# Recommendation tower on one core: two features of 26 go from gathers to lookups, and the gathers are released in another place

## The reference

```python
e = jnp.stack([tbl_0[ids[:, 0]], ..., tbl_25[ids[:, 25]]], axis=1)        # (2048, 26, 128)
combined = jnp.concatenate([dense[:, None, :], e], axis=1)                 # (2048, 27, 128)
interactions = jnp.einsum('bfd,bgd->bfg', combined, combined)
z = jnp.concatenate([dense, interactions[:, _IU0, _IU1]], axis=1)
h = jnp.concatenate([z, dense], axis=1)
h = jnp.maximum(h @ W_top1 + b_top1, 0.0)      # (607, 512)
h = jnp.maximum(h @ W_top2 + b_top2, 0.0)      # (512, 256)
y = h @ W_top3                                 # (256, 1)
```

## Time and profile before

| | |
|---|---|
| median of three timed runs | 380.81 us |
| span of the profiled execution | 496.1 us |
| its own time beside the span | not given with this profile |
| TensorE busy | 376.0 us, 3360 matmuls |
| weight loads | 301.4 us |
| DVE busy | 244.4 us |
| ACT busy | 195.0 us |
| GpSimd busy | 254.8 us, 256 of its 266 instructions gathers |
| mean granted TensorE clock | 0.904 of 2.4 GHz |
| moved by DMA | 58.44 MB, 118 GB/s on average |

### The profile page before, as it was taken

The page is one execution under the profiler, slowest core; times in us unless marked ns, Lnnn a source line. Parts: engine busy times, 40 slices in busy tenths (PEclk is TensorE's granted clock), DMA queues, the critical chain, the costliest instruction groups (busy, mean ns, idle before and its releaser), DMA issues.

```text
span 496.1 us, 8109 instructions
## 1 busy us (share of the span) xinstructions
PE 376.0 (76%) x3360; PEld 301.4 (61%) x3360; DVE 244.4 (49%) x174; ACT 195.0 (39%) x261; POOL 254.8 (51%) x266
## 2 busy tenths in 40 slices
PE   1951777858586665978798796969788696879997
PEld 1630656647474554767586666867676455666787
DVE  4740789674919370765725750956566101112133
ACT  3810986414242521525252532434354334344400
POOL 6774540655737363646666554747466564730000
PEclk9985799989989796989998898989899898789899
DMA  8841763259915153456714533536232621123330
GB/s 210 218 134 41 218 187 85 70 156 275 227 29 161 45 155 103 109 150 153 183 46 128 160 87 104 143 93 193 74 89 63 168 73 27 49 63 100 69 71 5
DMA packets 38479, 58.44 MB, mean 118 GB/s; under 512 B 21665, under 2 KB 22561, under 8 KB 38444
## 3 DMA queue, kind: packets, MB, share of 16 engines
q1 hardware_dynamic: 29304, 40.74, 30.3%
q0 software_dynamic: 8192, 16.79, 13.5%
q10 hardware_dynamic: 948, 0.41, 0.4%
HBM read 47.68 MB, written 10.23 MB: 117 GB/s over the span
## 4 chain that ended last, share of the span: by engine, by line
PE 58%; issue 16%; DVE 11%; another core or an unknown queue 8%; SPq 3%; DMA 2%; ACT 2%; DVEq 0%; ACTq 0%
PE look_bank L727 25%; PE short_bank L821 15%; DVE one_hot L1031 8%; PE out_bank L757 6%; PE out_bank L771 4%; PE short_bank L806 4%; PE out_bank L766 3%; SPq L632 2%; DVE all_combined L1044 1%; DVE low_table L1019 1%; DMA spread_ids<-in_ids_by_feature 1%; PE out_bank L783 1%; SPq L621 1%; DMA last_scratch<-all_dots 1%
## 5 line engine op out<-in xcount | busy, mean ns | idle before, releaser
L682 POOL DMA_INDIRECT rows<-in_tbl,all_ids x256 | 253.9, 992 | 191.9 <-PE short_bank L821 81.9
L1031 DVE TENSOR_TENSOR one_hot<-spread_ids,row_bank 128x2048 fp32r<-128x2048 int32 (+3 forms) x80 | 170.7, 2175 | 27.1 <-PE look_bank L727 10.7
L727 PE MATMUL look_bank<-one_hot,high_table 125*128 125x512 f32 x328 | 140.8, 429 | 20.0 <-issue 16.1
L727 PE MATMUL look_bank<-one_hot,low_table 125*128 125x512 f32 x328 | 132.4, 404 | 0.6 <-issue 0.6
L821 PE MATMUL short_bank<-all_combined 128*59 128x54 f32 x2048 | 88.1, 247 | 53.2 <-issue 51.5
L821 PEld LDWEIGHTS short_bank<-all_combined 128*59 128x59 f32 x2048 | 79.7, 162 | 66.7 <-issue 66.5
L1044 DVE COPY all_combined<-short_bank 128x512 f32<-128x512 f32 x32 | 21.8, 691 | 156.2 <-PE short_bank L806 122.3
L727 PEld LDWEIGHTS look_bank<-one_hot,high_table 125*128 125x128 f32 x328 | 64.5, 197 | 40.5 <-issue 23.6
L727 PEld LDWEIGHTS look_bank<-one_hot,low_table 125*128 125x128 f32 x328 | 64.6, 197 | 16.9 <-issue 4.1
L925 ACT COPY all_dots<-short_bank 128x432 f32<-128x432 f32 x64 | 33.1, 518 | 97.1 <-remote 53.7
L878 ACT COPY looked_up<-look_bank 128x512 f32<-128x512 f32 x40 | 23.4, 586 | 120.8 <-remote 45.3
(11 more groups left out here) (42 smaller groups left out, 183.5 us busy)
## 6 DMA issues: line engine op xcount, KB each, us to landing
whole_table<-in_tbl SPq DMA_DIRECT2D x26, 448.0 KB
spread_ids<-in_ids_by_feature SPq DMA_DIRECT2D x40, 256.0 KB
block_scratch<-all_dots SPq DMA_DIRECT2D x24, 208.0 KB
rows<-in_tbl,all_ids POOLq DMA_INDIRECT x256
block_scratch<-all_dots SPq DMA_DIRECT2D x24, 104.0 KB
pairs<-block_scratch SPq DMA_DIRECT2D x72, 29.2 KB
whole_table<-in_tbl SPq DMA_DIRECT2D x26, 52.0 KB
whole_table<-in_tbl SPq DMA_DIRECT2D x2, 560.0 KB
```

What stands on the lines that cost most here:

```text
L682: nc.gpsimd.indirect_dma_start(rows[:, t % ROW_TILES, slot, :], None, tables[SLOT_FEATURES[slot]][:, :], bass.IndirectOffsetOnAxis(ap=all_ ...
L727: last = nc.tensor.matmul(look_bank[s % LOOK_BANKS][:], table_parts[part][TABLE_PLACE[s]][0:ROWS_K, c, :], one_hot[0:ROWS_K, (chunks_befor ...
L1031: last = nc.vector.tensor_tensor(one_hot[:, place:place + n, :], spread_ids[:, s % ID_PLACES:s % ID_PLACES + 1, :].to_broadcast([P, n, COLS]),
```

## The change

Two more features of every block are looked up: 14 gathered, 12 looked up. The order of slots changes so that three tables of 1250 rows are among the twelve. Places shrink to 18 for one-hots and 5 for ids, and grow to 20 for looked-up results. Each tile's stage gets six halves of lookups. The transposes of tile 0 stand behind eight lookups, not four. The groups of slots are 4, 4, 4 and 2. The gathers of tile 2 are released by the transposes of tile 0; behind these a table, `GATHERS_BESIDE`, says how many gathers of the tiles 3 to 15, in order, follow the transposes of tile 1, of tile 2, and so on. No gather waits for dots or for halves of lookups.

```diff
-SLOT_FEATURES = [6, 3, 10, 23, 2, 4, 8, 11, 12, 13, 14, 15, 16, 18, 19, 21, 1, 5, 7, 9, 17, 20, 0, 22, 24, 25]
+SLOT_FEATURES = [6, 3, 10, 23, 2, 4, 8, 11, 12, 13, 14, 15, 16, 18, 1, 5, 7, 19, 9, 17, 20, 21, 22, 24, 25, 0]
-GATHERED = [16, 16, 16, 16]
+GATHERED = [14, 14, 14, 14]
-HOT_PLACES = 20
-ID_PLACES = 7
-LOOK_PLACES = 15
+HOT_PLACES = 18
+ID_PLACES = 5
+LOOK_PLACES = 20
-GROUPS = [[4, 4, 4, 4] for _ in range(BLOCKS)]
+GROUPS = [[4] * (n // 4) + [n % 4] * (n % 4 > 0) for n in GATHERED]
-HALVES_AFTER = [[6, 5, 5, 4] for _ in range(LAST)]
+HALVES_AFTER = [[6, 6, 6, 6], [6, 6, 6, 6], [6, 6, 6, 6]]
-LOOKS_BEFORE_TURN = 4
+LOOKS_BEFORE_TURN = 8
-HIGH_BEFORE_TURN = 6
-HIGH_PAIR = 6
-def high_after(s):
-    if s == HIGH_BEFORE_TURN - SPLIT_AHEAD or s == HIGH_PAIR + 1:
-        return []
-    return [s + SPLIT_AHEAD, s + SPLIT_AHEAD + 1] if s == HIGH_PAIR else [s + SPLIT_AHEAD]
+GATHERS_BESIDE = [11, 11, 11, 11] + [15] * 8 + [10, 8]
+TILES_AT_START, TILES_BEFORE_DOTS = 2, 3
+def gathers_beside(w):
+    rest = [(t, slot) for t in range(TILES_BEFORE_DOTS, TILES) for slot in range(GATHERED[t // PER_BLOCK])]
+    first = sum(GATHERS_BESIDE[:w])
+    return rest[first:first + GATHERS_BESIDE[w]]
...
 def look_place(s):
-    return BLOCK_OF[s] % 2 * (LOOK_PLACES - IN_BLOCK[0]) + LOOK_SLOT[s]
+    return BLOCK_OF[s] % 2 * (LOOK_PLACES - IN_BLOCK[BLOCK_OF[s]]) + LOOK_SLOT[s]
...
-            for t in range(ROW_TILES):
-                gather(t, range(n_groups(t)))
-            for t in range(TILES - ROW_TILES):
-                pool.wait_ge(turned_done, groups_by(t))
-                gather(t + ROW_TILES, range(1))
-                for g in range(1, n_groups(t + ROW_TILES) - 1):
-                    if 0 < t <= LAST * PER_BLOCK:
-                        pool.wait_ge(half_done, halves_beside(t, g))
-                    gather(t + ROW_TILES, range(g, g + 1))
-                pool.wait_ge(dots_done, (t + 1) * FILLS - 1)
-                gather(t + ROW_TILES, range(n_groups(t + ROW_TILES) - 1, n_groups(t + ROW_TILES)))
+            for t in range(TILES_AT_START):
+                gather_tile(t)
+            pool.wait_ge(turned_done, groups_by(0))
+            for t in range(TILES_AT_START, TILES_BEFORE_DOTS):
+                gather_tile(t)
+            for w in range(len(GATHERS_BESIDE)):
+                pool.wait_ge(turned_done, groups_by(w + 1))
+                for t, slot in gathers_beside(w):
+                    gather(t, slot)
```

More of the change, by code:

```diff
@@ L108 @@
 ACT_HOTS = [1, 2, 4, 5, 7, 8]
-LOOKS_BEFORE_TURN = 4
+LOOKS_BEFORE_TURN = 8
 START_IDS_AHEAD = 5
 DENSE_AFTER = 1
-HIGH_BEFORE_TURN = 6
-HIGH_PAIR = 6
-def high_after(s):
-    if s == HIGH_BEFORE_TURN - SPLIT_AHEAD or s == HIGH_PAIR + 1:
-        return []
-    return [s + SPLIT_AHEAD, s + SPLIT_AHEAD + 1] if s == HIGH_PAIR else [s + SPLIT_AHEAD]
+GATHERS_BESIDE = [11, 11, 11, 11] + [15] * 8 + [10, 8]
+TILES_AT_START, TILES_BEFORE_DOTS = 2, 3
+assert sum(GATHERS_BESIDE) == sum(GATHERED[t // PER_BLOCK] for t in range(TILES_BEFORE_DOTS, TILES))
+def gathers_beside(w):
+    rest = [(t, slot) for t in range(TILES_BEFORE_DOTS, TILES) for slot in range(GATHERED[t // PER_BLOCK])]
+    first = sum(GATHERS_BESIDE[:w])
+    return rest[first:first + GATHERS_BESIDE[w]]
 def group_slots(t, g):
@@ L150, in odds_by, with group_of @@
     return sum(n_groups(i) // 2 for i in range(t + 1))
+def group_of(t, slot):
+    return next(g for g in range(n_groups(t)) if slot in group_slots(t, g))
 def turn_use(t, g):
@@ L184, in look_place, with block_before @@
 def look_place(s):
-    return BLOCK_OF[s] % 2 * (LOOK_PLACES - IN_BLOCK[0]) + LOOK_SLOT[s]
+    return BLOCK_OF[s] % 2 * (LOOK_PLACES - IN_BLOCK[BLOCK_OF[s]]) + LOOK_SLOT[s]
+def block_before(s):
+    earlier = [BLOCK_OF[i] for i in range(s) if look_place(i) == look_place(s)]
+    return earlier[-1] if earlier else None
 def chunks_before(s):
@@ L216, in hots_by_dve @@
     return half + 1 - hots_by_act(half)
-def halves_beside(t, g):
-    before = 2 * IN_BLOCK[0] + sum(HALVES_AFTER[i // PER_BLOCK][i % PER_BLOCK] for i in range(t - 1))
-    return before + 1 + (g - 1) * HALVES_AFTER[(t - 1) // PER_BLOCK][(t - 1) % PER_BLOCK] // 2
 def free_places(half):
@@ L678, in _, with gather, gather_tile @@
         def _(pool):
[L679 to L684, removed]
+            def gather(t, slot):
+                nc.gpsimd.indirect_dma_start(
+                    rows[:, t % ROW_TILES, slot, :], None, tables[SLOT_FEATURES[slot]][:, :],
+                    bass.IndirectOffsetOnAxis(ap=all_ids[:, t, slot:slot + 1], axis=0)).then_inc(
+                        gathered[t % ROW_TILES][group_of(t, slot)], 16)
+            def gather_tile(t):
+                for slot in range(GATHERED[t // PER_BLOCK]):
+                    gather(t, slot)
             nc.gpsimd.memset(ones[:], 1.0).then_inc(ones_ready, 1)
@@ L873, in copy_look @@
             def copy_look(s):
-                if s >= LOOK_PLACES:
-                    act.wait_ge(look_moved, moves_by(BLOCK_OF[s - LOOK_PLACES] * PER_BLOCK + PER_BLOCK - 1))
+                if block_before(s) is not None:
+                    act.wait_ge(look_moved, moves_by(block_before(s) * PER_BLOCK + PER_BLOCK - 1))
                 act.wait_ge(half_done, 2 * (s + 1))
@@ L966, in copy_ends @@
                         m = BLOCK_OF[s]
-                        for ahead in high_after(s):
-                            high_part(ahead)
+                        high_part(s + SPLIT_AHEAD)
                         if s == FIRST_MOVES[0] - 1:
@@ L986, in _ @@
             copy_ends(start[:LOOKS_BEFORE_TURN])
-            high_part(HIGH_BEFORE_TURN)
             copy_dense(0)
```

## The result

The changed kernel takes 418.6 us (median of 5 runs, 417.78 to 422.99) against 380.5 us before (378.82 to 381.22). The ratio is 1.1022, with a 95% interval of 1.0968 to 1.1075: 38 us slower. Forecast were 410 us and a range of 393 to 420.

A forecast was written before the change was run, and what follows sets the result against it. TensorE's work and the start were taken to bound the kernel, GpSimd close behind. Lookups +36.4, transposes -4.1, start +4, gather order -8, DVE +1 summed to +29, so 380.8 became 410 us; range 393 to 420.

The forecast's parts named there:

- The ledger of TensorE's work: Kernel before: TensorE's matmuls and transposes, added up from trace rows at full clock, come to 323 us.
- the 53 us and the 81 us: TensorE, kernel before: 53 us of work taking longer and 81 us of issue idle, which timed runs can't have.
- TensorE's work and the start are thus the bound: Kernel before: 323 us of work plus 52 of the other 57 us named, about 5 us unnamed.
- GpSimd was the bound: Rival, kernel before: gathers bind, all 24 us of the loop's idle would go, 396 us; chance 0.24.
- chain of 371 us: GpSimd, kernel before: gathers from the first dots end at 339 us, 31.5 us follow, 10 us under the median.
- Lookups, +36.4: TensorE's lookups: 80 more chunks, 160 matmuls of 0.2275 us, counting in full, +36.4 us.
- Start, +13.1: Up to first dots: DVE's four new halves and two low parts; 9.1 us matmuls, +4 beyond, bounds 0 and +8.
- the 14 us I took out: Start, kernel before: ACT's standstill of 21.65 us for a lookup's copy; without 14 us, first dots at 70.7 us.
- The order of the gathers, -8: Loop: fewer gathers beside dots end stalls; the timed run gets back between 0 and 5 plus 19 us, taken as -8.
- DVE in the loop, +1: Loop: DVE 18.0 us a tile against TensorE's 18.3 in block 0, hidden in others; +1, bounds 0 and +9.
- DVE becomes the bound: Rival, changed kernel: 46 us more DVE work delays copies, 1.5 us in each of 12 tiles, 427 us; chance 0.10.
- TensorE's lookups waiting for DVE's one-hots in the loop: Sign of a wrong forecast: with a time over 420 us, these waits would mean DVE.

The follow-up runs named there:

- the second profile: Kernel before, unchanged, profiled once more: 380.0 us, span 377.5 us.
- the first profile: Profile of the kernel before that the prediction used: span 496.1 us; the timed runs it cites have a median of 380.8 us.
- The run with more matmuls: Kernel before with the matmuls of two lookups in each block made twice, 144 more: 403.5 us, ratio 1.0591.
- the run with less of DVE: Changed kernel with DVE's one-hot comparisons of each block's last two lookups over 64 columns, not 512: 409.3 us, ratio 1.0781.
- old release: Changed kernel with gathers released as before, behind transposes, halves of lookups and the third bank of dots: 418.1 us, ratio 1.0959.
- ACT's halves: Changed kernel with the second halves of the one-hots of lookups 10 and 11 made by ACT, not DVE: 419.7 us, ratio 1.1010.
- early transposes: Changed kernel with the transposes of tile 0 behind four lookups, not eight: 418.4 us, ratio 1.0991.

## Why the prediction was right, step by step

**The ledger of TensorE's work.** 323 us forecast from rows at full clock; the second profile has 334.9 us busy. Of the 12 between them a part is matmuls at the lower level (a granted clock of 0.92 in tile 3); how much is not shown. That the 53 us and the 81 us of the first profile can't be in the timed runs was right: they are absent from the second profile (issue idle 2.1 us in all).

**What bounds the kernel before.** "TensorE's work and the start are thus the bound" was half right. The gather queue ran without a pause and held TensorE for 7.1 us; 28 gathers taken off gave 9. The rival "GpSimd was the bound" had its mechanism right, and I had worked with 1.25 us a gather from one stretch, where the mean of the whole queue is 1.33; its chain of 371 us also had the first dots 10 us too late. Measured, the chain is 377.5 us, the whole span. The rival's own time, 396 us, was far off, since it let all 24 us of the loop's waits go and 7 to 9 went. My argument against it ("no transpose in the trace waits for a gather") came from the profile whose stalls gave the queue time to catch up: there it waited 110 us for dots and transposes.

**Lookups, +36.4.** The matmuls keep their 0.227 us. In blocks 1 and 2, where TensorE is busy throughout, 16.2 us of matmuls less transposes were added and 13.5 appear; the rest filled idle time of TensorE, 4.1 us of which had been waits for rows. "They count in full" was thus a little too much. The run with more matmuls points the same way, with seven tenths of them showing; the runs with fewer give no price.

**Start, +13.1 (9.1 of matmuls and 4 beyond).** Measured +16.9, so 7.8 beyond, at the upper bound given. Where the first dots stand was wrong: 70.7 us forecast for before, 60.5 measured, since the first profile's start had lost more than the 14 us I took out. The cause was named rightly: DVE makes the last one-hots, and the run with less of DVE brings the first dots 6.6 us earlier. TensorE's idle time up to the first dots grows by 4.6 us; the rest of the 7.8 is longer busy time. DVE's time line of the changed kernel, which answers to the earlier trace rows:

```profile
62.41 5.08 DVE L1035 TENSOR_TENSOR one_hot<-spread_ids,row_bank 128x1024 fp32r<-128x1024 int32 x3
67.41 1.48 DVE L1023 TENSOR_TENSOR low_table<-whole_table,high_table 125x1280 fp32r<-125x1280 f32 x1
68.81 12.73 DVE L1035 TENSOR_TENSOR one_hot<-spread_ids,row_bank 128x2560 fp32r<-128x2560 int32 x6
```

The dots behind it, which answer to the earlier trace rows:

```profile
77.44 3.59 PE L827 MATMUL short_bank<-all_combined 128*59 128x54 f32 x125 [2.01 <-ACT all_combined L903]
```

Lookup 9 is copied out at 61.4 us (59.2 before), lookup 11 at 75.5.

**The order of the gathers, -8.** The size is near the 7.1 us of waits for rows that went, the reason is not. No stall beside gathers was there to remove, and the new order did nothing in either kernel. It was the number of gathers that ended the waits, which I had priced at nothing. That the two errors cancel is luck.

**DVE in the loop, +1.** This is the term that was mis-sized most. Block 0 grew by 16.3 us, of which the matmuls less transposes are 8.1: some 8 more, 2 a tile. Some 4 of them are busy time beyond the added work, at a granted clock of 0.92 to 0.93 in three of the four tiles (one of the four before), and some 4 are idle time. The run with less of DVE gives back 6.6 of the 8. I had seen 18.0 us of DVE against 18.3 of TensorE and called it even. DVE is busy for 74.4 of the 87.3 us, and it waits 11.4 us for lookup matmuls to free its places for one-hots (4.8 before). So neither is the bound alone; each waits for the other. No lookup waits for DVE in block 0: TensorE waits there for DVE's copies (6.6 us, 6.2 before) and for ACT's copies of looked-up results (4.2, 2.9 before). Whether the fewer places for one-hots (18, not 20), which the change brings too, have a share in this no run here tests. The rival "DVE becomes the bound" was in part right for the start and block 0, and wrong for blocks 1 and 2, where the run with less DVE changed no tile.

The Trainium skill (TensorE: Matmul & The Clock Gate, "HAM oscillation — how this bites in real kernels") tells of a kernel whose matmuls wait for loads that such a wait drops the array's clock and that the next matmuls start cold. The time line of tile 6 above agrees, though the wait there is for a copy: 3.27 us of waiting, and six microseconds at half speed behind it.

**The sum.** With measured terms: 36.4 - 4.1 for the work, +7.8 start, +8.2 block 0, -2.7 in blocks 1 and 2 (16.2 forecast by the work, 13.5 measured), -3.9 in the last tiles (-4.7 less the transposes' -0.8), +0.6 at the end: +42.3 us for the 42.6 between the spans of 377.5 and 420.1; the medians are 38 apart, and the spans of the four other runs of the changed kernel are 415.6 to 417.0 us. In the profiles of three runs that change next to nothing in its time (old release, ACT's halves, early transposes) the first dots and block 0 take 163.1 to 164.2 us, 31.5 to 32.6 more than before, so that both terms hold there to 2 us; block 1 takes 89.2 us in each. Of my +29, +4 and +1 should have been +8 and +8. Against that, 410 us lies 8.6 below the measured time, and the range held it with 1.4 us to spare: its upper end came from a part of the rival "DVE becomes the bound", and without that the range ended at 418.

**What would show it.** 816 matmuls and dots in one piece came as said, and so did the idle of GpSimd, though with 12 us at the start and not some 20. "TensorE's lookups waiting for DVE's one-hots in the loop" do not appear; what DVE costs appears in the start, and in block 0 as waits for copies and at the lower clock. No transpose waits for gathers.

## What to carry to other kernels

When a profile's span is far above the timed runs, add up the work at full clock and believe the difference to the timed median, but take no pattern of waiting from that profile, least of all that some queue is never late: a second profile of the same kernel costs little and turned that finding round. When work moves from a saturated queue to an engine and its supplier, price three terms, the engine's own work, the waits that end, and the coupling to the supplier; if both have equal lengths per tile, as in block 0 here, add something per tile (here 2 us), not nothing. And check a bound by adding work as well as by removing it: removal opened holes, and waiting and the lower clock took the gain away.

## What the runs showed of the hardware that I had not expected

Two profiles of one kernel differed by 119 us of span (496.1 and 377.5), with 81 us of "issue" idle behind the first matmul in the first and 2 in the second, while all timed runs of that kernel lie between 378.2 and 384.5 us. Removing 160 of 816 lookup matmuls at 0.227 us each made the changed kernel no faster (418.7 to 425.6 against 418.6 us), with a mean granted clock of 0.923 to 0.938 against 0.976 to 0.988. A stream of gathers of 128 rows took 1.25 us a piece in one stretch and 1.33 on average over 256 (341 us). Gathers beside dots cost the dots nothing that can be told: in the changed kernel with the old release most dots take 3.7 us like those with the new one.
